# Experts stage of a graph network kernel: two buffers for the turned rows, turned at block 5, and finished rows sent a chunk later

## Chip, cores and metric

The kernel runs on one core of a Trainium2 chip. The metric is the device time of one execution in microseconds (us); lower is better. Engine names: PE is TensorE's matrix multiplication and PEld its weight load, DVE is VectorE, ACT is ScalarE, POOL is GpSimd.

## What is computed

Four layers follow one another on 12,500 nodes of 256 features, each added to its input. The change touches the last one only: a mixture of 8 experts with top-1 routing and a capacity.

```python
def _L1_ffn_ref(h, gate_w, gate_b, w1, b1, w2, b2):
    ...
    logits = x @ gate_w + gate_b
    probs = jax.nn.softmax(logits, axis=-1)
    idx = jnp.argmax(probs, axis=-1)
    ...
    buf = jnp.zeros((E, C, D), dtype=h.dtype).at[idx, pos_safe].set(x, mode='drop')
    hmid = jax.nn.relu(jnp.einsum('ecd,edf->ecf', buf, w1) + b1[:, None, :])
    ybuf = jnp.einsum('ecf,efd->ecd', hmid, w2) + b2[:, None, :]
    y_tok = ybuf[idx, pos_g] * (prb * kept)[:, None]
    ...
    y = jnp.nan_to_num(y, nan=0.0, posinf=10000.0, neginf=-10000.0)
    return y
...
    x = x + _L1_ffn_ref(_layernorm(x, axis=-1)[None], ...)[0]
```

## The kernel before

The stage before has written one row of 513 numbers for each node to HBM (`routed`: normalised features, features, routing weight) and lists which node sits in which slot of which expert. The function `experts` then works through **chunks** of 256 slots (`TC`), in order of the experts; how many chunks an expert has is read from `chunks` at run time. This input gives 37 chunks (experts with 2, 2, 8, 4, 8, 2, 8 and 3). The first chunk of an expert stands alone in the program; its other chunks are one loop. Each engine has its own program over all chunks (`all_experts`) with its own chunk number `g` in a register, and the engines meet at semaphores.

Every product is taken in two parts: a number is rounded to a high part and a low part remains, and three products (high by low, low by high, high by high) are added. For one chunk `g`:

- **POOL** `fetch(g)` (L2309, L2313): copies the 2 x 128 row numbers into `of_row`, then fetches the rows into `XG` with two indirect DMAs. It waits until `XG` is free: its 256 features turned (`T_ok`) and the rest copied away (`r_in`). `send(g)` (L2320) then scatters finished rows `YR` to the output with two indirect DMAs, once they are ready (`row_ok`). POOL runs fetch, send, fetch, send, and so on.
- **PE** `turn` (L2428): four transposes of `XG` into the PSUM tile `ps_t`. `layer1(m)` (L2439, six matmuls) makes block `m` of 8 of the hidden layer, `layer2(m)` (L2450, six matmuls) adds that block's share to the result; `layer2` runs three blocks behind (`AHEAD`). The rows of chunk g+1 are turned in chunk `g`, ahead of `layer1(7)`.
- **ACT** applies bias and ReLU to each block (L2533, a high and a full copy). After block 7 it copies `ps_t` to `XT.high` (`turned_high`, L2482), and then the features and weight of chunk g+1 from `XG` to `XB` (`keep`, L2488), which waits for `r_free`. Only the end of `keep` lets POOL begin the fetch of the next rows.
- **DVE** makes the low part of each block (L2398) and, one step after each block, finishes the rows of the chunk before (`finish`, L2371 to L2383: weight, clip, NaN handling, residual). Its last step writes `YR` and releases `r_free` and `row_ok`. After that come `turned_low` (L2355) and the addition of the bias of layer 2 into `Y` (L2408).

In the first chunk of an expert, ACT and DVE also split the next expert's weights, a piece after each block (L2478, L2351). Seven of the first chunks do so.

What the prediction's steps rest on in code: PE begins a chunk with `pe.wait_ge(xT_low, g + 1)`; ACT's `keep(c)` is `s.wait_ge(r_free, c + 1)` and a copy that raises `r_in`; POOL's `fetch(g)` has `gp.wait_ge(r_in, g + 1)`. There is one `XG`, one `ps_t`, one `XT` and one `YR`, and two `XB`.

Of the kernel before, what the change touches and what calls it, by code (L numbers as in the profile page):

```python
# [6 lines left out]
FP32 = mybir.dt.float32  # L7
# [10 lines left out]
P = 128  # L18
# [2187 lines left out]
def experts(nc, a, k, scratch, out, ctx, sem, sbuf, psum):  # L2206
# [5 lines left out]
    WP = WF // PIECES  # L2212
    RH = 4
    AHEAD = 3
    stage = [sbuf(ctx, f"xw_stage{i}", [P, WF]) for i in pair]
    W = [Split(sbuf, ctx, f"xw{i}", [P, WF]) for i in pair]
    b2 = sbuf(ctx, "xb2", [P, NX, D])
# [4 lines left out]
    XB = sbuf(ctx, "xXB", [P, 2, CT, XW - D])  # L2222
    of_row = sbuf(ctx, "xof_row", [P, CT], I32)
    of_out = sbuf(ctx, "xof_out", [P, CT])
    XT = Split(sbuf, ctx, "xxT", [P, KB, TC])
    hid = Split(sbuf, ctx, "xhid", [P, RH, TC])
    hid_full = sbuf(ctx, "xhid_full", [P, RH, TC])
    Y = sbuf(ctx, "xY", [P, CT, D])
# [66 lines left out]
    with nc.Block() as block:  # L2295
# [5 lines left out]
        @block.gpsimd  # L2301
        def _(gp):
            def fetch(g, column):

                gp.wait_ge(T_ok, g + 1)
                hold(gp, passed)
                gp.wait_ge(r_in, g + 1)
                hold(gp, passed)
                gp.tensor_copy(of_row[:, :], k["row_of"][:, bass.ds(column, CT)]).then_inc(of_ok, 1)  # L2309
                gp.wait_ge(of_ok, g + 1)  # L2310
                hold(gp, passed)
                for j in range(CT):
                    gp.indirect_dma_start(out=XG[:, j, :], out_offset=None, in_=scratch["routed"],  # L2313
                                          in_offset=bass.IndirectOffsetOnAxis(ap=of_row[:, j:j + 1], axis=0)).then_inc(fetched, 16)

            def send(g):
                gp.wait_ge(row_ok, g + 1)
                hold(gp, passed)
                for j in range(CT):
                    gp.indirect_dma_start(out=out, out_offset=bass.IndirectOffsetOnAxis(ap=tok[:, j:j + 1], axis=0),  # L2320
                                          in_=YR[:, j, :], in_offset=None,
                                          bounds_check=N - 1, oob_is_err=False).then_inc(sent, 16)

            def chunk(g, column, e, par, first):
                fetch(g, column)
                send(g)
            done = all_experts(gp, "x_pool", nothing, chunk, nothing)
            g = gp.snap(done, min_val=1, max_val=MOST)
            fetch(g, 0)
            send(g)  # L2330
            send(g + 1)
            gp.wait_ge(sent, g * (16 * CT) + 2 * 16 * CT)

        @block.vector
        def _(v):
            v.sem_inc(y_ok, 1)
            nc.vector.memset(Y[:, :, :], 0.0).then_inc(blank, 1)
            nc.vector.memset(XB[:, 1, :, :], 0.0).then_inc(blank, 1)
            nc.vector.memset(YR[:, :, :], 0.0).then_inc(blank, 1)
            nc.vector.memset(of_out[:, :], float(FAR)).then_inc(out_ok, 1)  # L2340
            v.wait_ge(b_T, 1)
            nc.vector.tensor_copy(b1T[:, :], ps_t[:, 0:NX * FB]).then_inc(b_ok, 1)
            v.wait_ge(blank, 3)
            v.wait_ge(out_ok, 1)
            nc.vector.tensor_copy(tok[:, :], of_out[:, :]).then_inc(row_ok, 1)
            v.sem_inc(r_free, 1)

            def lower(par, n, ready):
                v.wait_ge(W_high, ready)
                high, low = W[par].at()  # L2350
                nc.vector.tensor_tensor(piece(low, n), piece(stage[par], n), piece(high, n).bitcast(FP32), SUB).then_inc(W_low, 1)  # L2351

            def turned_low(at):
                v.wait_ge(xT_high, at)
                nc.vector.tensor_tensor(XT.low[:, :, :], ps_t[:, :].rearrange("p (b t) -> p b t", b=KB),  # L2355
                                        XT.high[:, :, :].bitcast(FP32), SUB).then_inc(xT_low, 1)

            def finish(g):

                n = [0]  # L2360

                def step(ins):

                    n[0] += 1
                    ins.then_inc(dv, 1)
                    v.wait_ge(dv, g * STEPS + n[0])

                def xb(lo, hi):
                    return XB[:, bass.ds((g + 1) % 2, 1), :, lo:hi].rearrange("p x t f -> p (x t) f")
                v.wait_ge(r_in, g + 1)  # L2370
                yield step(nc.vector.tensor_tensor(Y[:, :, :], Y[:, :, :], xb(D, D + 1).to_broadcast([P, CT, D]), MUL))  # L2371
                yield step(nc.vector.tensor_scalar(C[:, :, :], Y[:, :, :], -BIGGEST, BIGGEST, MAX, MIN))
                yield step(nc.vector.tensor_tensor(odd[:, :, :], C[:, :, :], Y[:, :, :], ALU.not_equal))
                yield step(nc.vector.tensor_tensor(num[:, :, :], Y[:, :, :], Y[:, :, :], ALU.is_equal))
                yield step(nc.vector.tensor_scalar(Z[:, :, :], C[:, :, :], -NN_INF, NN_INF, MAX, MIN))
                yield step(nc.vector.tensor_tensor(Z[:, :, :], Z[:, :, :], num[:, :, :], MUL))  # L2376
                hold(v, passed)
                yield step(nc.vector.copy_predicated(C[:, :, :], odd[:, :, :], Z[:, :, :]))  # L2378

                v.wait_ge(sent, g * (16 * CT) + 16 * CT)  # L2380
                v.wait_ge(out_ok, g + 1)
                step(nc.vector.tensor_copy(tok[:, :], of_out[:, :]))
                nc.vector.tensor_tensor(YR[:, :, :], C[:, :, :], xb(0, D), ADD).then_inc(row_ok, 1)  # L2383
                v.wait_ge(row_ok, g + 2)
                v.sem_inc(r_free, 1)
                yield

            for n in range(PIECES):
                lower(0, n, n + 1)
            turned_low(1)  # L2390
            v.wait_ge(b2_in, 16)

            def chunk(g, column, e, par, first):
                last = finish(g)
                for m in range(FB):
                    v.wait_ge(h_ok, g * FB + (m + 2))
                    hold(v, passed)
                    nc.vector.tensor_tensor(hid.low[:, m % RH, :], hid_full[:, m % RH, :],  # L2398
                                            hid.high[:, m % RH, :].bitcast(FP32), SUB).then_inc(h_low, 1)
                    if first:  # L2400
                        lower(1 - par, m, (e + 1) * PIECES + (m + 1))
                    next(last)
                nc.vector.tensor_copy(of_out[:, :], k["out_of"][:, bass.ds(column, CT)]).then_inc(out_ok, 1)
                turned_low(g + 2)
                v.wait_ge(y_ps, g + 2)
                hold(v, passed)
                for j in range(CT):
                    ins = nc.vector.tensor_tensor(Y[:, j, :], ps_y[j][:, 0:D], b2[:, bass.ds(e, 1), :].rearrange("p x d -> p (x d)"), ADD)  # L2408
                ins.then_inc(y_ok, 1)
                v.wait_ge(y_ok, g + 2)  # L2410
            done = all_experts(v, "x_dve", nothing, chunk, nothing)
            for _ in finish(v.snap(done, min_val=1, max_val=MOST)):
                pass

        @block.tensor
        def _(pe):
# [16 lines left out]
                pe.wait_ge(W_low, e * PIECES + PIECES)  # L2433
                hold(pe, passed)

            def layer1(par, m):
                steps = [(x, y, b) for b in range(KB) for x, y in ((0, 1), (1, 0), (0, 0))]
                for n, (x, y, b) in enumerate(steps):
                    last = nc.tensor.matmul(ps_h[m % RH][:, 0:TC], w1_at(par, x, b, m), XT.at(b)[y],  # L2439
                                            start=n == 0, stop=n == len(steps) - 1)  # L2440
                last.then_inc(h_ps, 1)

# [11 lines left out]
            def chunk(g, column, e, par, first):  # L2454
                pe.wait_ge(xT_low, g + 1)
                hold(pe, passed)
                for m in range(FB + AHEAD):
                    if m == FB - 1:
                        turn(g * 32 + 64)
                    if m < FB:  # L2460
                        layer1(par, m)
                    if m >= AHEAD:
                        layer2(g, par, m - AHEAD)
                pe.wait_ge(l2_ok, g * FB + FB + RH)
# [5 lines left out]
        def _(s):  # L2470
# [6 lines left out]
            def raise_(par, n):  # L2477
                nc.scalar.copy(piece(W[par].high, n), piece(stage[par], n)).then_inc(W_high, 1)  # L2478

            def turned_high(at):  # L2480
                s.wait_ge(T_ok, at)
                nc.scalar.copy(XT.high[:, :, :].rearrange("p b t -> p (b t)"), ps_t[:, :]).then_inc(xT_high, 1)  # L2482

            def keep(c):
                s.wait_ge(fetched, c * (16 * CT) + 16 * CT)
# [9 lines left out]
            s.wait_ge(W_low, PIECES)  # L2495
            load(2, 0)
            s.wait_ge(b_ok, 1)
            turned_high(2)
            keep(0)

            def before(e, i, par, g):
# [25 lines left out]
            def chunk(g, column, e, par, first):  # L2527
                for m in range(FB):
                    s.wait_ge(h_ps, g * FB + (m + 1))
                    s.wait_ge(l2_ok, g * FB + (m + 1))  # L2530
                    hold(s, passed)
                    for part in (hid.high, hid_full):
                        ins = nc.scalar.activation(part[:, m % RH, :], ps_h[m % RH][:, 0:TC], ACT.Relu, bias=b1[par][:, m:m + 1])  # L2533
                    ins.then_inc(h_ok, 1)
                    if first:
                        raise_(1 - par, m)
                turned_high(g + 3)
                keep(g + 1)

            def after(e, i, par, left):  # L2540
# [36 lines left out]
```

## Time and profile before

| what | value |
|---|---|
| time, median of 3 runs | 6248.97 us (6247.11 to 6253.21) |
| time of the profiled execution | 6250.95 us |
| its span, first to last instruction | 6249.3 us |
| mean granted TensorE clock | 0.897 |
| experts stage, first layer-1 matmul to the span's end | 5687.4 to 6249.3 us |

Times of rows count from the span's start. In a row of the timeline, the first number is the start, the second the duration; what stands in brackets is how long the engine was idle before and what ended that. A row's line number is that of the kernel before.

### The profile page before, as it was taken

What the parts mean: (1) busy time and instruction counts of PE and PEld (TensorE: products, weight loads), DVE (VectorE), ACT (ScalarE), POOL (GpSimd) and SP (SyncE); (2) the same over time, 40 slices, a digit from 0 to 9 for tenths busy, and PEclk for the clock granted to TensorE, in tenths of its full rate; (3) what the DMA queues carried; (4) which work ended last, traced back from release to release, by engine and by line L of the source; (5) the groups of instructions that cost most, each with busy time, mean ns of one, the idle gap of its engine ahead of it and who ended that gap; (6) DMA issues with size and microseconds to landing.
All of it is one profiled execution on the core that took longest, in us unless ns stands there. A gap on an engine that the chain in (4) does not pass through costs nothing. (4 is left out here: it accounts for less than half of the span.)

```text
span 6249.3 us, 102386 instructions
## 1 busy us (share of the span) xinstructions
PE 4928.5 (79%) x33929; PEld 4410.6 (71%) x33930; DVE 4061.6 (65%) x10205; ACT 1780.0 (28%) x4090; POOL 4157.3 (67%) x4057
## 2 busy tenths in 40 slices
PE   4427999999999999999995666666666666666887
PEld 3326999999999999999994555555555555555887
DVE  5526988898888889888984343443443443435776
ACT  2302444444444444444441000000000000003554
POOL 1347777777777777777754777777777777771323
PEclk9658999999999999999997888878878877887999
DMA  6655555555555565555543555555555555553221
GB/s 183 167 145 144 150 147 149 152 148 148 149 151 149 147 150 150 147 148 154 147 106 91 133 139 137 133 143 134 134 142 134 134 142 134 139 132 106 82 63 51
DMA packets 610386, 848.90 MB, mean 136 GB/s; under 512 B 251280, under 2 KB 424418, under 8 KB 609276
## 3 DMA queue, kind: packets, MB, share of 16 engines
q0 software_dynamic: 181728, 505.88, 30.9%
q1 hardware_dynamic: 384538, 275.47, 17.5%
q10 hardware_dynamic: 43650, 61.62, 2.9%
q8 instruction: 254, 4.16, 0.3%
q14 instruction: 216, 1.77, 0.1%
HBM read 728.24 MB, written 116.75 MB: 135 GB/s over the span
## 5 line engine op out<-in xcount | busy, mean ns | idle before, releaser
L1234 POOL DMA_INDIRECT m_ring<-tab_a,m_src x1764 | 1989.0, 1128 | 672.3 <-issue 504.0
L1856 POOL DMA_INDIRECT eb_rows<-tab_b,eb_src x1764 | 1740.5, 987 | 541.1 <-issue 537.0
L2100 PE MATMUL eb_acc<-eb_rows,eb_S 128*128 128x257 f32 x3528 | 1076.2, 473 | 439.8 <-DMA eb_rows<-tab_b,eb_src 438.6
L2100 PEld LDWEIGHTS eb_acc<-eb_rows,eb_S 128*128 128x128 f32 x3528 | 842.3, 244 | 635.7 <-DMA eb_rows<-tab_b,eb_src 468.6
L1515 PE MATMUL m_acc<-m_V,m_S 128*128 128x264 f32 x3528 | 862.1, 390 | 0.0
L1515 PEld LDWEIGHTS m_acc<-m_V,m_S 128*128 128x128 f32 x3528 | 646.9, 192 | 93.4
L1909 DVE TENSOR_TENSOR eb_sum<-eb_acc,eb_sum 128x257 f32<-128x257 f32 x98 | 41.8, 426 | 1009.1 <-PE eb_acc L2100 1009.1
L1636 ACT ACTIVATE mh_high<-m_ps,bn_b,bn_s 128x256 fp32r<-128x256 f32 x784 | 441.4, 563 | 747.9 <-PE m_ps L537 744.8
L525 DVE TENSOR_TENSOR mh_low<-mh_full,mh_high 128x512 fp32r<-128x512 f32 x784 | 544.5, 695 | 107.7 <-ACT mh_full L1636 61.4
L1625 ACT ACTIVATE mh_full<-m_ps,bn_b,bn_s 128x256 f32<-128x256 f32 x784 | 400.6, 563 | 674.6 <-DVE mh_low L525 355.1
L1309 DVE TENSOR_TENSOR m_V<-m_ring,m_V 128x1280 f32<-128x1280 f32 (+1 forms) x392 | 532.7, 1359 | 13.4
L2184 ACT COPY rGT<-r_ps_g 128x512 f32<-128x512 f32 x98 | 52.6, 589 | 1449.8 <-PE r_ps_g L2110 1449.8
L1636 ACT ACTIVATE mh_full<-m_ps,bn_b,bn_s 128x256 f32<-128x256 f32 x784 | 441.2, 563 | 0.0
L1416 DVE SCALAR_TENSOR_TENSOR macc<-m_psY,mwg,macc 128x256 f32<-128x256 f32 x784 | 341.2, 477 | 61.8 <-PE m_psY L537 61.8
L537 PE MATMUL m_ps<-mXT_low,mW_high 128*128 128x256 f32 x1568 | 375.8, 321 | 0.0
L1891 DVE TENSOR_TENSOR eb_S<-eb_nodes,eb_dst 128x1152 f32<-128x1152 f32 x196 | 257.5, 1355 | 158.2 <-DMA eb_dst<-dst_p 156.5
L537 PE MATMUL m_psY<-mWo_low,mh_high 128*128 128x256 f32 x1568 | 344.2, 301 | 7.0 <-DVE macc L1416 6.9
L537 PE MATMUL m_ps<-mh_low,mW_high 128*128 128x256 f32 x1568 | 318.5, 284 | 3.1 <-DVE mh_low L525 1.7
L537 PE MATMUL m_psY<-mWo_high,mh_low 128*128 128x256 f32 x1568 | 312.9, 280 | 0.0
L537 PE MATMUL m_ps<-mXT_high,mW_low 128*128 128x256 f32 x1568 | 312.5, 281 | 0.0
L537 PE MATMUL m_psY<-mWo_high,mh_high 128*128 128x256 f32 x1568 | 312.1, 280 | 0.0
L537 PE MATMUL m_ps<-mXT_high,mW_high 128*128 128x256 f32 x1568 | 311.8, 280 | 0.0
(388 smaller groups left out, 10221.1 us busy)
## 6 DMA issues: line engine op xcount, KB each, us to landing
m_dstb<-dst_p SPq DMA_DIRECT2D x196, 320.0 KB
m_dstb<-dst_p SPq DMA_DIRECT2D x196, 256.0 KB
m_ring<-tab_a,m_src POOLq DMA_INDIRECT x1764
eb_rows<-tab_b,eb_src POOLq DMA_INDIRECT x1764, 2.8
routed<-rXR ACTq DMA_DIRECT2D x49, 513.0 KB, 8.7
xw_stage<-in_L_ffn_w_dram ACTq DMA_DIRECT2D x16, 1024.0 KB, 8.4
over<-b_blank SPq DMA_DIRECT2D x9, 1452.0 KB, 15.4
mOV<-over SPq DMA_DIRECT2D x49, 264.0 KB, 4.8
```

Of the source, the lines that this page charges most:

```text
L525: return nc.vector.tensor_tensor(low, full, high.bitcast(FP32), SUB)
L537: last = nc.tensor.matmul(out, x[i], y[j], start=n == 0, stop=n == len(steps) - 1)
L1234: gp.indirect_dma_start(out=ring[:, j, :], out_offset=None, in_=scratch["tab_a"], in_offset=bass.IndirectOffsetOnAxis(ap=src[:, j:j + 1], ...
L1309: nc.vector.tensor_tensor(to[:, 0:size, 0:D].rearrange("p t (h o) -> p t h o", h=H), got[:, :, 0:D].rearrange("p t (h o) -> p t h o", h=H) ...
L1416: nc.vector.scalar_tensor_tensor(acc[p][:, j, :], psY[:, j * D:(j + 1) * D], wg[p][:, j, e:e + 1], acc[p][:, j, :], MUL, ADD).then_inc(y_o ...
L1515: last_i = nc.tensor.matmul(ps_acc[s.par][:, 0:NA], S[:, s.first + j, :], V[s.side][:, j, :], start=s.first + j == 0, stop=s.first + j == ...
L1625: ins = nc.scalar.activation(hf1[:, m, :], ps1[:, m * T2:(m + 1) * T2], ACT.Relu, bias=bn_b[0][:, c:c + 1], scale=bn_s[0][:, c:c + 1])
L1636: ins = nc.scalar.activation(part[:, m, :], ps2[:, m * T2:(m + 1) * T2], ACT.Relu, bias=bn_b[1][:, c:c + 1], scale=bn_s[1][:, c:c + 1])
L1856: gp.indirect_dma_start(out=rows_[q.par][j][:, t, 0:D], out_offset=None, in_=scratch["tab_b"], in_offset=bass.IndirectOffsetOnAxis(ap=src_ ...
L1891: return nc.vector.tensor_tensor(to, numbers[:, :].rearrange("p (x n) -> p x n", x=1).to_broadcast([P, n, P]), dst.rearrange("p (t y) -> p ...
L2100: last_i = nc.tensor.matmul(ps_acc[j][:, 0:NR], S[q.par][j][:, t, :], rows_[q.par][j][:, t, :], start=t == 0, stop=t == WT - 1)
L2184: nc.scalar.copy(GT_[:, j, :, :].rearrange("p b t -> p (b t)"), ps_g[j][:, :]).then_inc(GT_ok, 1)
```

## The change

`XT` gets a second buffer. Chunk `g` reads buffer `g % 2`, chosen by a register on PE, ACT and DVE. All three turn the rows of chunk g+1 at block 5 (`TURN`): PE ahead of `layer1(5)`, ACT ahead of the activation of block 5, DVE after block 5 and its step of `finish`. A second increment of `row_ok` ahead of the loop lets POOL's `send(g)` carry what `finish(g - 2)` wrote, where it carried that of `finish(g - 1)`; so in POOL's order the send of the same rows now stands behind the next fetch. `YR` is still one buffer, and `finish` waits for the sends up to that later one. One more send stands at the end. `keep`, `XG`, `ps_t` and the condition of `fetch` stay.

```diff
--- before.py
+++ after.py
@@ -2212,6 +2212,7 @@
     WP = WF // PIECES
     RH = 4
     AHEAD = 3
+    TURN = 5
     stage = [sbuf(ctx, f"xw_stage{i}", [P, WF]) for i in pair]
     W = [Split(sbuf, ctx, f"xw{i}", [P, WF]) for i in pair]
     b2 = sbuf(ctx, "xb2", [P, NX, D])
@@ -2222,7 +2223,7 @@
     XB = sbuf(ctx, "xXB", [P, 2, CT, XW - D])
     of_row = sbuf(ctx, "xof_row", [P, CT], I32)
     of_out = sbuf(ctx, "xof_out", [P, CT])
-    XT = Split(sbuf, ctx, "xxT", [P, KB, TC])
+    XT = Split(sbuf, ctx, "xxT", [P, 2, KB, TC])
     hid = Split(sbuf, ctx, "xhid", [P, RH, TC])
     hid_full = sbuf(ctx, "xhid_full", [P, RH, TC])
     Y = sbuf(ctx, "xY", [P, CT, D])
@@ -2329,7 +2330,8 @@
             fetch(g, 0)
             send(g)
             send(g + 1)
-            gp.wait_ge(sent, g * (16 * CT) + 2 * 16 * CT)
+            send(g + 2)
+            gp.wait_ge(sent, g * (16 * CT) + 3 * 16 * CT)
 
         @block.vector
         def _(v):
@@ -2343,6 +2345,8 @@
             v.wait_ge(blank, 3)
             v.wait_ge(out_ok, 1)
             nc.vector.tensor_copy(tok[:, :], of_out[:, :]).then_inc(row_ok, 1)
+            v.wait_ge(row_ok, 1)
+            v.sem_inc(row_ok, 1)
             v.sem_inc(r_free, 1)
 
             def lower(par, n, ready):
@@ -2350,10 +2354,10 @@
                 high, low = W[par].at()
                 nc.vector.tensor_tensor(piece(low, n), piece(stage[par], n), piece(high, n).bitcast(FP32), SUB).then_inc(W_low, 1)
 
-            def turned_low(at):
-                v.wait_ge(xT_high, at)
-                nc.vector.tensor_tensor(XT.low[:, :, :], ps_t[:, :].rearrange("p (b t) -> p b t", b=KB),
-                                        XT.high[:, :, :].bitcast(FP32), SUB).then_inc(xT_low, 1)
+            def turned_low(c):
+                v.wait_ge(xT_high, c + 1)
+                low, high = (x[:, bass.ds(c % 2, 1), :, :].rearrange("p x b t -> p (x b t)") for x in (XT.low, XT.high))
+                nc.vector.tensor_tensor(low, ps_t[:, :], high.bitcast(FP32), SUB).then_inc(xT_low, 1)
 
             def finish(g):
 
@@ -2377,17 +2381,17 @@
                 hold(v, passed)
                 yield step(nc.vector.copy_predicated(C[:, :, :], odd[:, :, :], Z[:, :, :]))
 
-                v.wait_ge(sent, g * (16 * CT) + 16 * CT)
+                v.wait_ge(sent, g * (16 * CT) + 2 * 16 * CT)
                 v.wait_ge(out_ok, g + 1)
                 step(nc.vector.tensor_copy(tok[:, :], of_out[:, :]))
                 nc.vector.tensor_tensor(YR[:, :, :], C[:, :, :], xb(0, D), ADD).then_inc(row_ok, 1)
-                v.wait_ge(row_ok, g + 2)
+                v.wait_ge(row_ok, g + 3)
                 v.sem_inc(r_free, 1)
                 yield
 
             for n in range(PIECES):
                 lower(0, n, n + 1)
-            turned_low(1)
+            turned_low(0)
             v.wait_ge(b2_in, 16)
 
             def chunk(g, column, e, par, first):
@@ -2400,8 +2404,9 @@
                     if first:
                         lower(1 - par, m, (e + 1) * PIECES + (m + 1))
                     next(last)
+                    if m == TURN:
+                        turned_low(g + 1)
                 nc.vector.tensor_copy(of_out[:, :], k["out_of"][:, bass.ds(column, CT)]).then_inc(out_ok, 1)
-                turned_low(g + 2)
                 v.wait_ge(y_ps, g + 2)
                 hold(v, passed)
                 for j in range(CT):
@@ -2433,10 +2438,11 @@
                 pe.wait_ge(W_low, e * PIECES + PIECES)
                 hold(pe, passed)
 
-            def layer1(par, m):
+            def layer1(g, par, m):
+                turned = (XT.high, XT.low)
                 steps = [(x, y, b) for b in range(KB) for x, y in ((0, 1), (1, 0), (0, 0))]
                 for n, (x, y, b) in enumerate(steps):
-                    last = nc.tensor.matmul(ps_h[m % RH][:, 0:TC], w1_at(par, x, b, m), XT.at(b)[y],
+                    last = nc.tensor.matmul(ps_h[m % RH][:, 0:TC], w1_at(par, x, b, m), turned[y][:, bass.ds(g % 2, 1), b, :].rearrange("p x t -> p (x t)"),
                                             start=n == 0, stop=n == len(steps) - 1)
                 last.then_inc(h_ps, 1)
 
@@ -2455,10 +2461,10 @@
                 pe.wait_ge(xT_low, g + 1)
                 hold(pe, passed)
                 for m in range(FB + AHEAD):
-                    if m == FB - 1:
+                    if m == TURN:
                         turn(g * 32 + 64)
                     if m < FB:
-                        layer1(par, m)
+                        layer1(g, par, m)
                     if m >= AHEAD:
                         layer2(g, par, m - AHEAD)
                 pe.wait_ge(l2_ok, g * FB + FB + RH)
@@ -2477,9 +2483,9 @@
             def raise_(par, n):
                 nc.scalar.copy(piece(W[par].high, n), piece(stage[par], n)).then_inc(W_high, 1)
 
-            def turned_high(at):
-                s.wait_ge(T_ok, at)
-                nc.scalar.copy(XT.high[:, :, :].rearrange("p b t -> p (b t)"), ps_t[:, :]).then_inc(xT_high, 1)
+            def turned_high(c):
+                s.wait_ge(T_ok, c + 2)
+                nc.scalar.copy(XT.high[:, bass.ds(c % 2, 1), :, :].rearrange("p x b t -> p (x b t)"), ps_t[:, :]).then_inc(xT_high, 1)
 
             def keep(c):
                 s.wait_ge(fetched, c * (16 * CT) + 16 * CT)
@@ -2495,7 +2501,7 @@
             s.wait_ge(W_low, PIECES)
             load(2, 0)
             s.wait_ge(b_ok, 1)
-            turned_high(2)
+            turned_high(0)
             keep(0)
 
             def before(e, i, par, g):
@@ -2529,12 +2535,13 @@
                     s.wait_ge(h_ps, g * FB + (m + 1))
                     s.wait_ge(l2_ok, g * FB + (m + 1))
                     hold(s, passed)
+                    if m == TURN:
+                        turned_high(g + 1)
                     for part in (hid.high, hid_full):
                         ins = nc.scalar.activation(part[:, m % RH, :], ps_h[m % RH][:, 0:TC], ACT.Relu, bias=b1[par][:, m:m + 1])
                     ins.then_inc(h_ok, 1)
                     if first:
                         raise_(1 - par, m)
-                turned_high(g + 3)
                 keep(g + 1)
 
             def after(e, i, par, left):
```

**DVE, end of a chunk in the loop, before.** `xYR` is the last step of `finish`, `xxT_low` is `turned_low`, `xY` adds the bias of layer 2.

```order
L2383 TENSOR_TENSOR xYR<-xC,xXB 128x512
L2384 REGISTER_ALU
L2403 ISA
L2403 COPY xof_out<-out_of 128x2
L2355 TENSOR_TENSOR xxT_low<-x_ps_t,xxT_high 128x512
L2408 TENSOR_TENSOR xY<-x_ps_y,xb 128x256 x2
```

DVE in the changed kernel, from the step of `finish` behind block 5 (`xZ` times `xnum`) on; the `xhid_low` that follow are those of blocks 6 and 7.

```order
L2380 TENSOR_TENSOR xZ<-xZ,xnum 128x512
L2358 REGISTER_ALU
L2360 ISA
L2360 TENSOR_TENSOR xxT_low<-x_ps_t,xxT_high 128x512
L2400 REGISTER_ALU
L2402 TENSOR_TENSOR xhid_low<-xhid_full,xhid_high 128x256
L2382 COPY_PREDICATED xC<-xodd,xZ 128x512
L2400 REGISTER_ALU
L2402 TENSOR_TENSOR xhid_low<-xhid_full,xhid_high 128x256
```

`turned_low` went from behind `xYR` to a place ahead of blocks 6 and 7, and so ahead of `xYR`.

**ACT, end of a chunk in the loop, before.** The activations are those of block 7; `xxT_high` is `turned_high`, `xXB` is `keep`.

```order
L2533 ACTIVATE xhid_high<-x_ps_h,xb 128x256
L2533 ACTIVATE xhid_full<-x_ps_h,xb 128x256
L2481 REGISTER_ALU
L2482 CAST xxT_high<-x_ps_t 128x512
L2485 ISA
L2486 REGISTER_ALU
L2488 ISA
L2488 COPY xXB<-xXG 128x514
```

ACT in the changed kernel: the place ahead of block 5, and then the end of the chunk.

```order
L2535 REGISTER_ALU
L2487 REGISTER_ALU
L2488 ISA
L2488 COPY xxT_high<-x_ps_t 128x512
L2541 ACTIVATE xhid_high<-x_ps_h,xb 128x256
L2541 ACTIVATE xhid_full<-x_ps_h,xb 128x256
```

```order
L2541 ACTIVATE xhid_high<-x_ps_h,xb 128x256
L2541 ACTIVATE xhid_full<-x_ps_h,xb 128x256
L2491 ISA
L2492 REGISTER_ALU
L2494 ISA
L2494 COPY xXB<-xXG 128x514
```

`turned_high` stands ahead of the activations of block 5; `keep` is still the last instruction of the chunk.

**PE, start of a chunk, in the changed kernel.** The rows before are the same matmuls without the four rows that are no matmuls.

```order
L2461 REGISTER_ALU
L2445 ISA
L2445 MATMUL x_ps_h<-xxT_low,xw_high 128x256
L2445 REGISTER_ALU
L2445 MATMUL x_ps_h<-xxT_high,xw_low 128x256
L2445 MATMUL x_ps_h<-xxT_high,xw_high 128x256
L2445 ISA
L2445 MATMUL x_ps_h<-xxT_low,xw_high 128x256
L2445 REGISTER_ALU
L2445 MATMUL x_ps_h<-xxT_high,xw_low 128x256
```

Four register instructions are new in each chunk, all in the first two groups of `layer1(0)`; the other matmuls stand as before.

## Rows read from the trace of the kernel before

**Rows 1.** Waits, 5690 to 6249 us: engine line, released by, total us, times, longest.

```profile
PEld x_ps_h L2439 <- issue: 49.5, 36, 2.4
PE x_ps_h L2439 <- DVE xxT_low L2355: 35.3, 32, 1.6
...
PE x_ps_t L2428 <- DMA xXG<-routed,xof_row: 15.8, 19, 2.5
```

**Rows 2.** Timeline of DVE, ACT and PE about chunk 20 of 0 to 36.

```profile
5987.01 0.69 DVE L2383 TENSOR_TENSOR xYR<-xC,xXB 128x512 f32<-128x512 f32 x1
5988.00 0.68 DVE L2355 TENSOR_TENSOR xxT_low<-x_ps_t,xxT_high 128x512 fp32r<-128x512 f32 x1
...
5987.99 0.62 ACT L2488 COPY xXB<-xXG 128x514 f32 x1 [1.30 <-DVEq L2385]
...
5989.04 0.36 PE L2439 MATMUL x_ps_h<-xxT_low,xw_high 128*128 128x256 f32 x1 [0.99 <-DVE xxT_low L2355]
...
5994.03 0.28 PE L2439 MATMUL x_ps_h<-xxT_low,xw_high 128*128 128x256 f32 x1
...
6002.11 0.36 PE L2439 MATMUL x_ps_h<-xxT_low,xw_high 128*128 128x256 f32 x1 [0.94 <-DVE xxT_low L2355]
```

**Rows 3.** Chain that ended last, chunk 14: start, us on the chain, what.

```profile
5899.75 0.70 DVE xYR L2383
...
5903.69 0.21 POOL xof_row L2309
...
5906.04 4.25 DMA xXG<-routed,xof_row
5910.34 0.65 PE x_ps_t L2428 x4
...
5913.47 0.70 DVE xYR L2383
5914.56 0.60 DVE xxT_low L2355
```

**Rows 4.** Timeline of ACT: copies that raise `r_in`, of chunks 17, 18 and 24.

```profile
5946.46 0.62 ACT L2488 COPY xXB<-xXG 128x514 f32 x1 [3.61 <-DVEq L2385]
...
5961.35 0.62 ACT L2488 COPY xXB<-xXG 128x514 f32 x1 [1.29 <-DVEq L2385]
...
6042.14 0.62 ACT L2488 COPY xXB<-xXG 128x514 f32 x1 [1.30 <-DVEq L2385]
```

**Rows 5.** Timeline of DVE in chunk 14, behind the step of block 5.

```profile
5910.06 0.68 DVE L2376 TENSOR_TENSOR xZ<-xZ,xnum 128x512 f32<-128x512 f32 x1
5910.98 0.42 DVE L2398 TENSOR_TENSOR xhid_low<-xhid_full,xhid_high 128x256 fp32r<-128x256 f32 x1 [0.23 <-DVE xZ L2376]
5911.32 0.76 DVE L2378 COPY_PREDICATED xC<-xodd,xZ 128x512 f32<-128x512 int32 x1
5912.83 0.43 DVE L2398 TENSOR_TENSOR xhid_low<-xhid_full,xhid_high 128x256 fp32r<-128x256 f32 x1 [0.75 <-ACT xhid_full L2533]
```

**Rows 6.** Timeline of ACT: a copy of 128x512 ahead of an activation.

```profile
5931.33 0.62 ACT L2478 CAST xw_high<-xw_stage 128x512 fp32r<-128x512 f32 x1
5931.84 0.48 ACT L2533 ACTIVATE xhid_high<-x_ps_h,xb 128x256 fp32r<-128x256 f32 x1
```

**Rows 7.** Timeline of ACT and POOL: the one fetch with no send ahead.

```profile
5686.45 0.62 ACT L2488 COPY xXB<-xXG 128x514 f32<-128x514 f32 x1
...
5687.32 0.18 POOL L2309 COPY xof_row<-row_of 128x2 int32 x1 [12.96 <-ACT xXB L2488]
```

**Rows 8.** Line L2313 (fetch), all 76: end row of the view.

```profile
DMA to landing us min/median/max: 3.3/3.6/7.9
```

**Rows 9.** Line L2488: the register work that ACT does for one address.

```profile
L2488 ACTq FUSED_REGOPS  x37: 91/93/113, 5705.3 to 6230.9; - x37
```

**Rows 10.** Stretches: us, busy of PE, PEld, DVE, ACT, POOL, then PEclk, DMA share, GB/s.

```profile
5938.60:5945.40 6.80, 4.33 (x33) 3.98 (x34) 5.79 (x13) 2.67 (x6) 0.00 (x0) 1.00 0.01 2
5945.40:5952.20 6.80, 5.40 (x26) 5.13 (x26) 4.01 (x9) 2.87 (x7) 3.74 (x4) 0.50 0.06 17
```

## Prediction

> **What bounds the kernel now.** I read the waits of the experts stage first, then the timeline about one start of a chunk, then the chain that ended last. The waits seem to offer two gains: PE waits 35.3 us for `xxT_low` ahead of `layer1` and 15.8 us for the fetched rows ahead of the transposes [rows 1]. The first is not what it seems. At chunk 20, `xxT_low` ended at 5988.68 (5988.00 + 0.68), and the first matmul came at 5989.04 after 0.99 us of idle; one chunk later, idle was 0.94 us [rows 2]. The result lay ready for 0.36 us, so something else ended that gap. The weight loads' own idle time at these places is put down to issue, 49.5 us in 36 cases [rows 1]: PE waits for its own last product, branches back and sets its registers. That takes its 0.9 us with or without `xxT_low`.
>
> The chain shows the loop that matters [rows 3]: `xYR` (DVE), then the sends (POOL), `of_row`, the fetch, 4.25 us to its landing, the transposes (PE), block 7, the next `xYR`. From 5899.75 to 5913.47 that is 13.72 us, one chunk. So in this chunk the fetch already sets the pace; where it lands sooner, PE does, at 13.07 us (5989.04 to 6002.11) [rows 2]. The mean of six chunks of one expert is (6042.14 - 5961.35) / 6 = 13.47 us [rows 4]. I use it for all 23 chunks that neither open an expert's loop nor split weights; of the others seven split weights and seven open a loop.
>
> **The change part by part.** *The start of a chunk.* With two buffers, `xxT_low` is there long before. The gap stays at its 0.9 us of issue, so I cost the gain at 0. Bounds: the 0.05 us by which 0.99 exceeds 0.94, and the whole 35.3 us (a rival, below).
>
> *Sends behind the next fetch.* POOL no longer sends between the end of `keep` and the fetch. The one fetch with no send ahead shows what remains: `keep` ends at 5687.07, `of_row` starts at 5687.32, 0.25 us later [rows 7]. Before, `of_row` came at 5903.69, 3.94 us after `xYR` began [rows 3]; now `keep` begins 0.98 us after `xYR` [rows 2], takes 0.62, and 0.25 follow: 1.85 us. The fetch starts 2.1 us earlier.
>
> *The turn two blocks earlier.* PE reaches block 5 at 5994.03, 4.99 us after the chunk's start [rows 2]. When can the rows be there? `keep` began at 5987.99. Then 0.62 + 0.25 us, 2.35 us from `of_row` to the second fetch (5903.69 to 5906.04) [rows 3], and the landing, 3.6 us as a median [rows 8] or 4.25 as in chunk 14. That gives 5994.8 to 5995.5: the fetch, though earlier, is 0.8 to 1.4 us late for the earlier turn. **`keep` was not moved**: it still waits for `r_free`, behind block 7 and `xYR`, so the fetch cannot begin before a chunk's end.
>
> *What the late turn pushes.* Followed once round, with L the start of the transposes:
> - L to the low part of the block behind the turn: 2.49 us in chunk 14 (5910.34 to 5912.83) [rows 3, 5]. Now `turned_high` stands ahead of the activation; a copy of that size delays it by 0.51 us [rows 6]. Low part of block 5 at L + 3.00.
> - Its step of `finish` 0.34 us later (5910.98 to 5911.32), and 0.92 us from that step to the next instruction (5910.06 to 5910.98) [rows 5]: `turned_low` at L + 4.26. It holds DVE 0.60 us, its share of the chain [rows 3]: low part of block 6 at L + 4.86.
> - The predicated copy 0.34 us later, and 0.76 us of it plus the pause of 0.23 [rows 5]: block 7 at L + 6.19. `xYR` follows 0.64 us later (5912.83 to 5913.47) [rows 3, 5]: L + 6.83.
> - `keep` 0.98 later, L + 7.81; `of_row` 0.87 after that, L + 8.68; second fetch 2.35 later, L + 11.03; landing 3.6 to 4.25, of which I take 3.9 because 3.6 is the median over first and second fetches and the second lands later in the chain. Next transposes: L + 14.95, say **15.0 us a chunk**, between 14.65 and 15.3.
>
> PE alone would come round in its 13.07 us, plus at most 0.8 us that `layer2(7)` would wait for block 7, which DVE now finishes later. That is 13.9, under 15.0, so the fetch sets the pace in every chunk, and PE should wait some 1.1 to 1.5 us for it at block 5. Cost: 23 x (15.0 - 13.47) = **+35 us**, between +27 and +42.
>
> *Chunks that open a loop*, seven: 14.89 us now (5946.46 to 5961.35) [rows 4]; the same round with a landing a little longer gives 15.0 to 15.3, so +0.1 to +0.4 each, taken as 0.2: +1.4 us. *Chunks that split weights*, seven: DVE is their bound (its block takes longer than PE's), so the wait for the fetch hides behind DVE. `turned_low`'s 0.60 us move ahead of `xYR`, so the fetch behind starts later by up to that; the same 0.60 us go away behind `xYR`. Between 0 and 0.6, taken as 0.4, because the round is tied to `xYR`: +2.8 us.
>
> *Registers.* Each chunk has four new register instructions on PE, one or two on ACT and DVE. ACT's cost 0.09 us each [rows 9]. PE's stand before block 5 and hide behind the wait there. I take 0; if two on ACT and two on DVE lie in the round, it is 0.36 us, 11 us over 30 chunks. That a matmul with an address in a register runs slower is not shown by any row; the 18 of `layer1(5)` to `layer1(7)` would be in the round. I leave it out and let the 11 us stand for both. *The extra send* at the end and `finish`'s wait for it: a send is issued right behind the fetch, two issues of about 1 us, and `xYR` comes almost 7 us after the landing of that fetch. I cost that wait at 0; the landing is its cover.
>
> **Sum.** 35 + 1.4 + 2.8 = 39 us on the profiled execution's 6250.95 us gives 6290. That execution lies 2 us above the median of the runs, so the forecast is **6288 us**, slower by 0.6%. By the bounds: +27 to 42 + 2.8 + 4.2 + 11 = +60, 6276 to 6309.
>
> **The rivals.** *The gap at the start goes* (faster). The same gap, chunk after chunk, on the engine that should be busy looks like a missing buffer, and the change adds it. If also the fetch kept up, 35.3 + 15.8 us would go: 6198 us. Decides: idle ahead of the first matmul falling well under 0.9 us. Against it stand the 0.36 us for which the result lay ready. Chance 0.05. The Trainium skill says in "Perfetto Trace Analysis" (Optimization Strategy) that consistent bubbles can mean that there is not enough memory for the next tile, a count of buffers; by that rule this rival would be the likeliest, and the trace does not agree at the start of a chunk, where the buffer had been filled 0.36 us before.
>
> *The fetch lands in time* (faster). From `keep` to block 5 there are 6.04 us (5987.99 to 5994.03) [rows 2]; the fetch needs 6.8 to 7.5. If without sends ahead it landed in under 2.8 us, the turn would not wait, and the 15.8 us of today's wait would go: 6233 us. But of 76 landings none took under 3.3 us [rows 8]. Chance 0.08.
>
> *The lateness does not feed back* (no change). If PE waits its 0.8 us at block 5 and DVE catches up, so that `xYR` keeps its distance from the chunk's start, a chunk costs 13.07 + 0.8 = 13.9: 23 x 0.4 = +9 us, 6258. Against it: DVE has one more step to make between the turn and `xYR`, not fewer. Chance 0.07.
>
> *The clock falls* (slower still). After a stretch in which PE was busy for 4.33 of 6.8 us at the full 2.4 GHz, the next 6.8 us ran at 0.50, which is 1.2 GHz [rows 10]. The new wait makes each chunk idler. At half speed `layer1(5)` to `layer1(7)` and the two `layer2` between, 3.5 us by the rows (0.70 us a group, 4.99 / 7), take 7; about 1 us of this hides behind DVE. If half the 30 chunks lost 2.5 us: +37 more, 6325. Chance 0.05.
>
> **How the numbers follow.** Forecast 0.75, the rivals 0.05, 0.08, 0.07 and 0.05. A difference under 0.2% (12.5 us) can't be told from none. Faster is 0.13, the same 0.07, slower 0.80. The range leaves out the two fast rivals and the slowest one (0.18): from 6254, which still holds the case without feedback, to 6314, the upper bound with a little for a clock that falls now and then.
>
> **What the changed profile would show.** Right: `keep` to `keep` near 15 us in the loops; PE's wait for `xXG` ahead of the transposes at about 30 to 45 us in place of 15.8; idle at the start of a chunk still at 0.9 us, put down to issue; `of_row` 0.25 us behind `keep`; PE waiting for `xhid_low` of block 7. Wrong: transposes at block 5 with no wait ahead; landings under 3 us; `xYR` less than 6.5 us behind the transposes; a start gap of a few tenths.

## The result: slower by 0.84%, and the profile after

The changed kernel takes 6302.69 us in the median (6299.19 to 6303.11, 4 runs), the one before 6249.89 us (6247.11 to 6253.21, 4 runs): ratio 1.0084, 95% interval 1.0070 to 1.0099. The profiled execution's span is 6301.3 us, against 6249.3 before.

PE's waits in the experts stage of the changed kernel, in the columns of [rows 1]:

```profile
PEld x_ps_h L2445 <- issue: 53.5, 36, 2.7
...
PE x_ps_h L2445 <- issue: 38.9, 28, 2.5
PE x_ps_y L2456 <- DVE xhid_low L2402: 28.5, 46, 1.5
...
PE x_ps_t L2433 <- DMA xXG<-routed,xof_row: 22.0, 23, 2.0
```

In the kernel before, the list has besides the lines of [rows 1]:

```profile
PE x_ps_y L2450 <- DVE xhid_low L2398: 16.4, 27, 1.0
```

The wait for `xxT_low` is no longer in the list, but its time is: the idle ahead of `layer1` is now put down to issue (the engine waited for nothing that the profile shows), 38.9 us against the 35.3 us that DVE was blamed for. The wait for the fetched rows grew from 15.8 to 22.0 us, and that for low parts of the hidden layer from 16.4 to 28.5 us; 18.3 us of it lie at block 7, for which PE now waits in each of the 37 chunks.

One start of a chunk and the round that follows it, chunk 7 and the first half of chunk 8, as a timeline of PE, ACT, DVE and POOL (compare [rows 2, 3, 5]):

```profile
5804.06 0.38 PE L2445 MATMUL x_ps_h<-xxT_low,xw_high 128*128 x1 [1.14 <-issue]
...
5809.80 0.44 PE L2433 MATMUL x_ps_t<-ident,xXG 128*128 128x128 f32 x2 [0.62 <-DMA xXG<-routed,xof_row]
...
5811.51 0.59 ACT L2488 CAST xxT_high<-x_ps_t 128x512 f32 x1 [2.05 <-PE x_ps_h L2445]
5811.99 0.48 ACT L2541 ACTIVATE xhid_high<-x_ps_h,xb 128x256 fp32r<-128x256 f32 x1
...
5812.98 0.42 DVE L2402 TENSOR_TENSOR xhid_low<-xhid_full,xhid_high 128x256 fp32r<-128x256 f32 x1 [1.19 <-ACT xhid_full L2541]
...
5814.25 0.69 DVE L2360 TENSOR_TENSOR xxT_low<-x_ps_t,xxT_high 128x512 f32 x1 [0.24 <-DVE xZ L2380]
5814.86 0.41 DVE L2402 TENSOR_TENSOR xhid_low<-xhid_full,xhid_high 128x256 fp32r<-128x256 f32 x1
...
5816.17 0.42 DVE L2402 TENSOR_TENSOR xhid_low<-xhid_full,xhid_high 128x256 fp32r<-128x256 f32 x1 [0.23 <-DVE xC L2382]
...
5816.81 0.69 DVE L2387 TENSOR_TENSOR xYR<-xC,xXB 128x512 f32<-128x512 f32 x1
...
5817.76 0.62 ACT L2494 COPY xXB<-xXG 128x514 f32 x1 [2.79 <-DVEq L2389]
...
5818.62 0.18 POOL L2310 COPY xof_row<-row_of 128x2 int32 x1 [8.81 <-ACT xXB L2494]
...
5818.83 0.38 PE L2445 MATMUL x_ps_h<-xxT_low,xw_high 128*128 x1 [1.14 <-issue]
...
5825.40 0.60 PE L2433 MATMUL x_ps_t<-ident,xXG 128*128 128x128 f32 x4
```

The clock in chunk 7 and at the start of chunk 8, in the columns of [rows 10]:

```profile
5804.06:5818.83 14.77, 12.55 (x101) 11.80 (x101) 9.52 (x21) 7.39 (x18) 4.21 (x5) 1.00 0.17 53
5819.20:5822.50 3.30, 3.30 (x18) 3.30 (x17) 1.03 (x2) 1.68 (x4) 2.26 (x3) 0.50 0.27 78
```

The reader is to see five things. The gap at the start is still there, 1.14 us, and its releaser is issue, though `xxT_low` had ended 3.89 us ahead of chunk 8 (5814.25 + 0.69 to 5818.83). PE stands idle 0.62 us for the fetch at block 5. `xxT_high` and `xxT_low` now lie between the transposes and `xYR`, which begins 7.01 us after them. And `of_row`, with which the next fetch begins, waits for `keep`, which waits for `xYR`. Of POOL's sends nothing is left ahead of it. Last, the fetch does not end every round: chunk 8 began at the lower clock (granted 0.50, which is 1.2 GHz), and PE came to its transposes 6.57 us after the chunk's start, where it was 5.74 in chunk 7, with no idle time ahead of them.

From start to start, a chunk in a loop takes 15.10 us in the mean, against 13.38 before. This mean, used below for every run, is over the 16 chunks that are neither the first of a loop, nor alone, nor an expert's last. In the changed kernel they are of three kinds. In nine, PE waited 0.5 to 0.7 us for the fetch: 14.75 us in the mean. In four (8, 10, 18 and 20), the chunk began at the lower clock and PE did not wait for the fetch at all: 15.55 us. In three (14, 22 and 32), the rows landed late and PE waited 1.1 to 1.6 us: 15.52 us; the rows of these three landed late in the kernel before too, 4.1 to 4.3 us after the second fetch began, where 3.5 to 3.7 us is usual.

### The profile page after: what moved, and what is told of

Read it like the earlier page. It is cut to its first block and busy times, and to the rows that moved or that the text cites. A ratio compares the mean times of both kernels' runs of the same rounds, so it can differ in the third digit from the quotient of the medians.

```text
span 6301.3 us, 102652 instructions
## 1 busy us (share of the span) xinstructions
PE 4959.7 (79%) x33929; PEld 4433.6 (70%) x33930; DVE 4064.2 (64%) x10205; ACT 1782.3 (28%) x4090; POOL 4146.2 (66%) x4059
```

## The experiments

Times are medians; the ratio is to the kernel before, measured beside the run: 6249.89 us for the change, 6245.04 us (25 runs) for e1 to e4, 6247.94 us (15 runs) for e5 to e8.

| run | us | ratio (95% interval) | chunk in a loop, us |
|---|---|---|---|
| before, in its profiled execution | 6250.95 | | 13.38 |
| the change | 6302.69 | 1.0084 (1.0070 to 1.0099) | 15.10 |
| e1_turn7 | 6257.65 | 1.0018 (1.0009 to 1.0028) | 13.58 |
| e2_sends_only | 6234.50 | 0.9980 (0.9971 to 0.9990) | 12.96 |
| e3_buffers_only | 6249.39 | 1.0008 (0.9998 to 1.0017) | 13.48 |
| e4_keep5 | 6300.09 | 1.0084 (1.0067 to 1.0101) | 15.08 |
| e5_copies_late | 6267.57 | 1.0031 (1.0019 to 1.0044) | 13.88 |
| e6_keep3 | 6277.90 | 1.0047 (1.0031 to 1.0064) | 14.04 |
| e7_keep3_copies_late | 6250.90 | 1.0005 (0.9995 to 1.0015) | 13.32 |
| e8_filler | 6299.32 | 1.0080 (1.0064 to 1.0097) | 14.93 |

**e3_buffers_only**: the kernel before with two `XT`, its copies and the turn where they were.

```diff
-    XT = Split(sbuf, ctx, "xxT", [P, KB, TC])
+    XT = Split(sbuf, ctx, "xxT", [P, 2, KB, TC])
...
-                    last = nc.tensor.matmul(ps_h[m % RH][:, 0:TC], w1_at(par, x, b, m), XT.at(b)[y],
+                    last = nc.tensor.matmul(ps_h[m % RH][:, 0:TC], w1_at(par, x, b, m), turned[y][:, bass.ds(g % 2, 1), b, :].rearrange("p x t -> p (x t)"),
```

> The kernel before with two buffers for the turned rows, picked by the register, and nothing else. Theory (the gap at a chunk's start is PE's own loop work, not the wait for the low part): nothing gained, 0.2 us of register work more at each of 37 starts: 6256 us, 6248 to 6264. Rival (the missing buffer makes the gap): the 35 us go, 6215 us, and the gap falls under 0.3 us.

Nothing is gained, and nothing that can be told from zero is lost. Timeline of DVE and PE at one start:

```profile
5990.18 0.69 DVE L2356 TENSOR_TENSOR xxT_low<-x_ps_t,xxT_high 128x512 f32 x1
...
5991.26 0.38 PE L2440 MATMUL x_ps_h<-xxT_low,xw_high 128*128 x1 [1.28 <-DVE xxT_low L2356]
```

The gap is 1.28 us where it was 0.94 to 0.99 [rows 2]. What ends it e3 alone can't tell: the copies stand where they stood, so `xxT_low` comes no earlier, and its end 0.39 us before the start is no sign of an idle result, since no start in e3 came less than 0.34 us after it. The changed kernel tells it: there `xxT_low` was ready 3.89 us ahead, and the gap was 1.14 us. So in a loop the gap is PE's own work between two chunks, with the new register instructions some 0.2 us longer. The rival that the missing buffer makes it falls; so does, for this gap, the reading of consistent bubbles in the Trainium skill ("Perfetto Trace Analysis", Optimization Strategy): the buffer was added and filled long ahead, and the bubble stayed. Where a loop opens it is different: at five of seven starts behind a chunk that splits weights, the gap fell from 1.40 to 1.56 us in the kernel before to 0.86 to 0.97 us in the changed one.

**e2_sends_only**: the kernel before with the four edits of the sends.

```diff
-                v.wait_ge(sent, g * (16 * CT) + 16 * CT)
+                v.wait_ge(sent, g * (16 * CT) + 2 * 16 * CT)
...
-                v.wait_ge(row_ok, g + 2)
+                v.wait_ge(row_ok, g + 3)
```

> The kernel before with the sends a chunk later and nothing else. Theory: the fetch starts 2.1 us sooner, PE's 15.8 us of waiting ahead of the transposes go, a chunk in a loop takes about 13.1 us: 6234 us, 6226 to 6242. Rival (the wait of the finish step for a send that now stands behind the fetch costs time): not under 6248 us.

6234.5 us: faster than both kernels. PE's wait for the fetched rows is gone from the list of waits, and two starts follow one another at 12.97 us:

```profile
5811.06 0.36 PE L2442 MATMUL x_ps_h<-xxT_low,xw_high 128*128 128x256 f32 x1 [0.99 <-DVE xxT_low L2358]
...
5824.03 0.35 PE L2442 MATMUL x_ps_h<-xxT_low,xw_high 128*128 128x256 f32 x1 [0.99 <-DVE xxT_low L2358]
```

The wait of `finish` for the later send costs nothing that shows.

**e1_turn7**: the change with one number put back.

```diff
-    TURN = 5
+    TURN = 7
```

> The change with the turn put back to block 7 (two buffers, registers and later sends stay). Theory (the fetch starts too late for a turn at block 5, and the copies stand ahead of the finished rows): rows land some 6 us after a chunk's start and are needed at 7.9 us, so no wait ahead of the transposes; about 0.2 us a chunk for the register work and 0.3 us of waiting for block 7 stay: 6250 us, 6240 to 6262. Rival (registers in the matmuls or the later sends cost the time): it stays above 6285 us.

6257.65 us, as expected. Each against its own kernel before, the change loses 53 us and e1 13, so 40 us of the loss come from the turn at block 5 and what moves with it. Against e2 the buffers and ACT's copy ahead of block 7 are left; a chunk in a loop takes 0.62 us more, of which the gap at the start is 0.2 us (1.20 against 0.99). Most of the rest is PE's wait for block 7's low part, which comes in all 37 chunks of e1 (16.6 us) and in 8 of e2 (7.3 us).

**e4_keep5**: the change with a third `XB`, and `keep` behind `turned_high` at block 5.

```diff
-                s.wait_ge(r_free, c + 1)
+                s.wait_ge(r_free, c if not isinstance(c, int) else 1)
...
                     if m == TURN:
                         turned_high(g + 1)
+                        keep(g + 1)
...
-                keep(g + 1)
```

> The change with a third buffer for the rest of the rows, so that the copy which lets the next fetch begin can follow the turn at block 5 and need not wait for the finished rows. Theory (the round from finished rows over the fetch to the transposes sets the pace): the fetch begins some 8 us earlier, PE waits under 3 us in all for it, a chunk in a loop takes 13.3 us: 6240 us, 6228 to 6255. Rival (DVE's longer line between turn and finished rows or the lower clock is the bound, not the fetch): above 6280 us.

The expectation was wrong by 60 us and the rival's bound held. No wait of PE for the fetch is left in the list, and the time is that of the change. What took its place stands first in the timeline of ACT at one block 5:

```profile
5814.56 0.62 ACT L2494 COPY xXB<-xXG 128x514 f32 x1
5815.08 0.48 ACT L2542 ACTIVATE xhid_high<-x_ps_h,xb 128x256 fp32r<-128x256 f32 x1
```

and then in PE's waits of the experts stage:

```profile
PE x_ps_y L2456 <- DVE xhid_low L2402: 48.7, 81, 1.5
PE x_ps_h L2445 <- issue: 38.9, 28, 2.6
```

`keep`, put ahead of block 5's activation, is a third copy between the turn and the finished block 7, and PE waits 48.7 us for low parts. Of the 16 chunks in a loop nine took 14.4 to 14.6 us and seven 16.0 to 16.1; the seven, and none of the nine, began at the lower clock. One such start (chunk 8, from 5821.97), with the stretch ahead of it, in the columns of [rows 10]:

```profile
5800.00:5822.00 22.00, 17.66 (x142) 16.57 (x140) 14.43 (x32) 10.18 (x26) 6.81 (x9) 1.00 0.19 60
5822.00:5825.40 3.40, 3.40 (x19) 3.40 (x20) 1.08 (x3) 1.68 (x4) 1.59 (x2) 0.62 0.22 77
```

I had taken the fetch for the only thing that a late turn costs, against my own sum, which has both copies in the line. So the next runs take the two causes apart. The lower clock at a chunk's start is a third, 1.5 us in each of these seven chunks.

**e6_keep3**: third `XB` and the freed `keep` as in e4, but `keep` still the chunk's last instruction on ACT.

```diff
...
-                s.wait_ge(r_free, c + 1)
+                s.wait_ge(r_free, c if not isinstance(c, int) else 1)
...
```

> The change with a third buffer for the rest of the rows, the copy that lets the next fetch begin left behind block 7, but without its wait for the finished rows. Theory of two causes: the fetch begins 2.6 us earlier and PE's wait for it goes, but the copies still hold up block 7, so PE waits for block 7's low part instead, about 14.1 us a chunk and more where the clock is low: 6290 us, 6275 to 6302. Rival (the late fetch is the only cause): 6245 us.

**e5_copies_late**: PE turns at block 5; `turned_high` stands behind block 7 ahead of `keep`, `turned_low` behind `xYR`.

```diff
-                    if m == TURN:
-                        turned_low(g + 1)
                 nc.vector.tensor_copy(of_out[:, :], k["out_of"][:, bass.ds(column, CT)]).then_inc(out_ok, 1)
+                turned_low(g + 1)
...
-                    if m == TURN:
-                        turned_high(g + 1)
...
+                turned_high(g + 1)
                 keep(g + 1)
```

> The change with PE's transposes at block 5, but ACT's and DVE's copies of the turned rows back behind block 7. Theory (two causes: the fetch is late for block 5, and the copies lie between the turn and the finished rows): the round loses the 0.5 us of ACT's copy and the 0.6 us of DVE's, 14.7 to 13.6 us a chunk; PE still waits for the fetch: 6272 us, 6260 to 6284. Rival (the copies' place does not matter, the fetch alone does): 6295 us or more.

**e7_keep3_copies_late**: both edits together.

> Both of the last two together: third buffer with the early copy, and ACT's and DVE's copies of the turned rows behind block 7. Theory of two causes: neither is left, PE sets the pace with its 13.1 us and 0.2 us of register work: 6245 us, 6235 to 6257. Rival (a third cause, such as matmuls with an address in a register or the transposes' place on PE): above 6270 us.

All three times lie in the ranges expected from two causes. PE's waits in e6, e5 and e7, one fence each:

```profile
PE x_ps_y L2456 <- DVE xhid_low L2402: 31.6, 51, 1.5
...
PE x_ps_t L2433 <- DMA xXG<-routed,xof_row: 0.5, 1, 0.5
```

```profile
PE x_ps_t L2432 <- DMA xXG<-routed,xof_row: 24.6, 29, 2.5
...
PE x_ps_y L2455 <- DVE xhid_low L2402: 10.7, 16, 1.0
```

```profile
PE x_ps_y L2455 <- DVE xhid_low L2402: 15.7, 22, 1.1
...
PE x_ps_t L2432 <- DMA xXG<-routed,xof_row: 2.1, 3, 1.7
```

With the fetch freed (e6), PE waits for low parts in place of rows; with the copies late (e5), for rows in place of low parts; with both (e7), for little of either, and the time is that of the kernel before. As a square of chunk times in a loop: 15.10 us with both causes, 14.04 without the late fetch, 13.88 without the copies in the line, 13.32 with neither. The two do not add up: 1.06 and 1.22 us alone, 1.78 together. In us of the whole, each run against its own kernel before: 23, 33 and 50 of the 53 lost. The lower clock went with them: of the 16 chunks, one began low in e6 (15.52 us, the others 13.86 to 14.05), and none in e5 and e7. A chunk of e7 still takes 0.36 us more than one of e2, nearly all of it in the gap at the start (1.31 against 0.99 us): in e2 PE waits for no rows any more, so nothing is left that an earlier turn could save.

**e8_filler**: the change with idle matmuls where PE waits for block 7's low part.

```diff
                     if m >= AHEAD:
+                        if m - AHEAD == FB - 1:
+                            for n in range(6):
+                                nc.tensor.matmul(ps_spare[:, 0:TC], w1_at(par, 0, 0, n), hid.at(0)[0], start=True, stop=True)
                         layer2(g, par, m - AHEAD)
```

> The change with six idle matmuls of 0.12 us each ahead of the last group of layer 2, where PE waits for the low part of block 7; their result is not used. Theory (the waits lower the clock, and low stretches at a chunk's start cost PE time): the time at the lower clock in this stage falls from 88 us to under 55 us and the time by about 10 us: 6292 us, 6282 to 6299. Rival (the lower clock hides behind the wait for the fetch): 6300 us or more, since nothing is gained and PE has 37 x 0.7 us more work.

The first half of the theory came true. Summed from the stage's first matmul to its last, the time at the low level is 21 us in place of 88 (40 in the kernel before). The same stretch of the change and then of e8:

```profile
5830.00:5970.00 140.00, 115.37 (x841) 109.39 (x840) 90.19 (x195) 71.19 (x169) 36.77 (x43) 0.91 0.23 75
```

```profile
5830.00:5970.00 140.00, 116.20 (x919) 110.78 (x918) 92.63 (x200) 71.77 (x172) 34.68 (x41) 0.98 0.24 78
```

The second half the medians leave open: 3 us less, or 1 us with each against its own kernel before, well inside both intervals. In the two profiled executions the stage alone, from its first layer-1 matmul, took 609.8 us in place of 618.3, near the gain expected; but that is one execution each, and the part ahead of the stage, which is the same program, took 7.3 us longer in that of e8. The chunks show more. Of the four in a loop that began low in the change (15.5 us each), three take 14.8 to 14.9 us here, and the fourth, whose rows landed late, 15.28. From `keep` to `keep`, the 23 chunks of the prediction's main term take 15.00 us in the mean in place of 15.25. PE's wait for the fetch went to 40.0 us:

```profile
PE x_ps_t L2434 <- DMA xXG<-routed,xof_row: 40.0, 35, 3.6
```

PE came sooner and waited longer. The filler in the waits kept the clock up, so the low clock of the changed kernel is a consequence of its waits, and a part of its cost hides behind the wait for the fetch: 0.8 us a chunk were left in the change, against 1.5 in e4, where PE has no such wait. In the chunks that began low in the change it did set the time.

## Why the prediction was right, and where its sizes were off

**The start gap, costed at 0**: right in the loops. It is 1.14 us and put down to issue, with `xxT_low` ready 3.89 us before. The evidence was weaker than the prediction took it to be: chunk 20, with its 0.36 us, was the widest case in a loop, and 15 of the 37 starts came 0.15 us after `xxT_low`, the least in that kernel. The result and PE's own work ended almost together. The gain of some 0.6 us at five openings of a loop was left out.

**The earlier fetch**: right. `of_row` began 1.80 us after `xYR` (5802.05 to 5803.85 on the rows of chunk 7; 1.85 predicted), and e2 shows what it is worth on its own, 10.5 us by the medians (6245.04 less 6234.50).

**The turn ahead of the fetch, with `keep` not moved**: right as a round, but not in every chunk. The steps of the round, from the transposes at 5809.80: block 5's low part +3.18 (3.00 predicted), `turned_low` +4.45 (4.26), block 6 +5.06 (4.86), block 7 +6.37 (6.19), `xYR` +7.01 (6.83), `keep` +7.96 (7.81), `of_row` +8.82 (8.68). The 0.18 us too much arise ahead of block 5 and stay; ACT's and DVE's register work lies there, the term that I set to 0 and kept in the bound, but no run takes it apart. The second fetch followed `of_row` as predicted, and the 12 chunks in a loop in which PE then waited took 14.94 us in the mean (14.95 predicted; its steps add up to 14.93): 14.75 with a usual landing, 15.52 with a late one.

That the fetch sets the pace in every chunk is the step that did not hold. PE waited for it at 23 of 37 turns, 22.0 us in all where 30 to 45 were forecast, and came to the other 14 with no wait ahead, which the prediction itself lists as a sign of being wrong. In four of the 16 chunks in a loop, and in eight of the 23 that the prediction priced alike, it was the lower clock at the start that made PE late.

**The price of a chunk in a loop** was the mis-sized term: +1.5 us predicted. From `keep` to `keep`, as the prediction counted, the 23 chunks took 15.25 us in the mean against 13.49, +1.76, so 40 us where 35 stood (one of these 23 opens the last expert's loop: eight chunks open a loop, not seven). The excess belongs to the lower clock, which the sum left out: in e8, where none of the 23 began low, they took 15.00 us, as predicted. **Chunks that open a loop and chunks that split weights** were sized far too small: 15.72 against 14.53 (+1.2, predicted +0.2) and 20.18 against 18.94 (+1.25, predicted +0.4; six with a chunk ahead), together 16 us where 4 stood. I took one opening chunk's 14.89 for all, which the mean of seven does not bear out, and took DVE's line for a cover in the others. The three make 56 us; 4.5 us go back because this execution came to the stage that much earlier (first matmul of the stage at 5682.97 against 5687.43), and the span grew by 52.

**The rivals.** The gap that goes, the fetch in time and the lateness without feedback did not come. The falling clock, given 0.05, came in part: the time at the low level went from 40 to 88 us and cost some 0.7 us in eight of the 23 chunks, far less than that rival's 2.5 us in half of 30. The range held, near its upper end.

That the loss has two causes was in the sum, but I did not draw it out: it says that PE's own line with the copies in it (13.9 by the prediction, 14.04 in e6) is only 0.7 us under the round that I called the bound (14.75 where PE waits for the usual landing). Freeing the fetch alone could therefore never give the gain back, as my expectation for e4 had it.

## What to carry to other kernels

Before a consumer is moved earlier, follow its input back to what starts the load: here the load hung on the end of the chunk before, and the earlier place only made it late. A copy that is moved to an earlier place is moved ahead of everything behind it on its engine; if something there feeds the loop, its length enters every round. And of a change with several parts try each alone: the parts that looked like its heart lost 40 us or gave nothing, and the small one, the order of sends and fetch on POOL, was worth 10 us.

## What was unexpected

A wait that the profile puts down to a producer can be the waiting engine's own work: 35.3 us of PE's waits were ended by `xxT_low` by the profile, and with the result ready 3.9 us ahead 38.9 us of idle time were still there, put down to issue. The time between the result's end and the next start is a weak sign of it: in the loops of the kernel before it was 0.15 to 0.36 us, and the gap was 0.94 to 1.00 us throughout. What told it was a kernel in which the result comes long before.

The lower clock costs what the wait behind it does not cover. A chunk in a loop that began low took 1.5 us more in e4, where no wait for a load was left, and 0.8 us more in the change, where PE would else have waited 0.5 to 0.7 us for its rows. In e8, where the clock stayed up, PE's wait for rows grew by 18 us, and the stage was 8.5 us shorter in the one profiled execution.
